# A graph network layer on one core: 21 dense blocks instead of 18, and all five extra groups built in the second layer

## The reference, cut to what matters

```python
xn = _layernorm(x)
deg_out = segment_sum(edge_weight, src); deg_in = segment_sum(edge_weight, dst)
norm = edge_weight * rsqrt(deg_out[src] * deg_in[dst] + EPS)
h6 = relu(segment_sum((xn @ W6)[src] * norm[:, None], dst) + b6)
h7 = relu(segment_sum((h6 @ W7)[src] * norm[:, None], dst) + b7)
gnn = h7 @ Wp + bp
q, k, v = xn @ wq.T, xn @ wk.T, xn @ wv.T      # 4 heads of 64; k and v are layer-normed
mix = (q @ (k.T @ v / S)) @ wo.T + bo
x = x + gnn + mix
x = x + ffn(_layernorm(x))                      # 2 of 8 experts, picked once for all nodes
```

## Time and profile before

| | |
|---|---|
| time, median of 3 runs | 3923.15 us (3919.55 to 3930.97) |
| span of the profiled execution | 3561.3 us |
| own time of the profiled execution | not listed apart from the three runs |
| PE busy | 2813.0 us (79%) |
| DVE busy | 1936.5 us (54%) |
| ACT busy | 950.0 us (27%) |
| POOL busy | 2357.1 us (66%) |
| moved by DMA | 511.33 MB, mean 144 GB/s |

### The profile page before, as it was taken

How to read it: one execution, slowest core, us unless ns; L and a number is a source line. 1 busy time by engine, 2 the same in 40 slices (tenths; PEclk the granted TensorE clock), 3 DMA queues, 4 the chain that set the end, 5 groups by cost and what they waited for, 6 DMA issues and landing times.

```text
span 3561.3 us, 51404 instructions
## 1 busy us (share of the span) xinstructions
PE 2813.0 (79%) x15774; PEld 1830.9 (51%) x15774; DVE 1936.5 (54%) x5283; ACT 950.0 (27%) x3210; POOL 2357.1 (66%) x2283
## 2 busy tenths in 40 slices
PE   4565558998989889998953577888778868869998
PEld 4454425555556555655521345555546535545666
DVE  9999846787778777877752142222243242232334
ACT  6787642332333323332220020000020010012111
POOL 5776577777777777777765777777777777730000
PEclk8788979999999999999975799999989999989999
DMA  4110035555555555555555546566646646642221
GB/s 132 59 44 1 2 104 151 167 159 151 162 164 158 150 157 170 155 156 160 166 177 156 170 149 195 197 201 200 195 147 196 197 153 193 198 156 95 79 71 49
DMA packets 260757, 511.33 MB, mean 144 GB/s; under 512 B 64843, under 2 KB 138459, under 8 KB 260141
## 3 DMA queue, kind: packets, MB, share of 16 engines
q0 software_dynamic: 97920, 268.62, 26.0%
q1 hardware_dynamic: 156057, 232.90, 19.7%
q10 hardware_dynamic: 6500, 6.40, 0.5%
HBM read 398.63 MB, written 109.15 MB: 143 GB/s over the span
## 4 chain that ended last, share of the span: by engine, by line
POOL 32%; PE 25%; DVE 15%; issue 12%; DMA 10%; SPq 4%; DVEq 1%; ACT 1%; ACTq 0%; POOLq 0%
POOL ringb L1908 31%; PE ps L676 7%; DVE ab L1058 6%; PE ps L845 5%; PE ps L858 5%; DMA ringb<-t,src 4%; PE ps L653 3%; DVE ab L1056 3%; DMA ab<-in_x 2%; SPq L1969 2%; PE ps L637 2%; SPq L1964 1%; DMA ab<-ad 1%; DMA rsd_in<-rdi 1%; POOL ab L1881 1%
## 5 line engine op out<-in xcount | busy, mean ns | idle before, releaser
L1908 POOL DMA_INDIRECT ringb<-t,src x2040 | 2044.2, 1002 | 684.0 <-issue 604.2
L676 PE MATMUL ps<-xb,ab 125*128 125x256 f32 (+1 forms) x4100 | 1062.0, 399 | 23.0 <-DMA ab<-ad 20.9
L676 PEld LDWEIGHTS ps<-xb,ab 125*128 125x128 f32 x4100 | 796.6, 199 | 287.1 <-issue 103.1
L653 PE MATMUL ps<-mlb 128*125 128x350 f32 x1176 | 495.6, 512 | 127.8 <-DVE mlb L1250 82.5
L637 PE MATMUL ps<-ringb,Sb 128*32 128x257 f32 (+1 forms) x4080 | 348.8, 416 | 280.6 <-DMA ringb<-t,src 178.2
L1697 ACT ACTIVATE ab<-ps 125x300 f32 x637 | 284.3, 446 | 671.0 <-PE ps L653 617.1
L559 PE MATMUL ps<-ab 128*50 128x125 f32 x3240 | 245.9, 306 | 183.3 <-ACT ab L1624 127.6
L1881 POOL TENSOR_TENSOR ab<-ab,wn 128x100 f32<-128x100 f32 x202 | 276.4, 1374 | 126.4 <-DVE ab L1056 126.4
L653 PEld LDWEIGHTS ps<-mlb 128*125 128x125 f32 x1176 | 208.6, 201 | 281.7 <-DVE mlb L1250 163.7
L637 PEld LDWEIGHTS ps<-ringb,Sb 128*32 128x32 f32 x4080 | 83.3, 111 | 496.7 <-DMA ringb<-t,src 273.7
L559 PEld LDWEIGHTS ps<-ab 128*50 128x50 f32 x3240 | 207.8, 143 | 221.2 <-DVE ab L1058 189.2
(11 more groups left out here) (231 smaller groups left out, 2520.8 us busy)
## 6 DMA issues: line engine op xcount, KB each, us to landing
ad<-ab SPq DMA_DIRECT2D x200, 312.5 KB
ab<-ad SPq DMA_DIRECT2D x200, 312.5 KB
ringb<-t,src POOLq DMA_INDIRECT x2040
x2t<-mlb SPq DMA_DIRECT2D x13, 500.0 KB, 18.5
xb<-x2t SPq DMA_DIRECT2D x13, 500.0 KB, 8.2
xb<-in_x SPq DMA_DIRECT2D x10, 625.0 KB
t<-xb SPq DMA_DIRECT2D x10, 625.0 KB
kvb<-t SPq DMA_DIRECT2D x50, 125.0 KB
```

The source lines that it names most:

```text
L653: e.matmul(PS[(2, 7, 4, 5)[bank_of(t)]][0:R, 0:HR], low[:, slot_of(t), :], high[:, slot_of(t), :], start=True, stop=True).then_inc(s_bld, 1)
L676: ins = e.matmul(PS[3][:, 0:wd], lhs, X[0:R, k, 0:wd], start=k == 0, stop=k == NT - 1)
L1908: e.indirect_dma_start(msg[:, slot * QT + k, 0:width], None, table, bass.IndirectOffsetOnAxis(src[:, t:t + 1], 0)).then_inc(s_g[slot], 16)
```

## The change

`ND`, the dense chunks of 30 tiles, goes from 18 to 21, and a block is begun every 11 steps instead of 13. The gathered groups fall from 45 to 41, so that the first layer has 246 steps with a gather instead of 270 and the second 216 instead of 240; the tiles fall from 1620 to 1614. The five extra groups are other ones, and all of them are built in the second layer, four tiles a step over six steps, instead of three of the five at three tiles a step over eight. The first layer builds 630 tiles instead of 588 (two or three a step both times) and runs 1050 dense products instead of 900; the second builds 120 instead of 72 and runs 1300 instead of 1150. 21 blocks are stored and loaded instead of 20. A chunk of the second layer has 176/26 = 6.8 steps instead of 206/23 = 9.0. Keys and values: of every fourth node tile phases 2 and 3 share a step, which takes them 237 steps instead of 250. `X_AT` comes to the steps 234, 236 and 240 (before 237, 240, 244), the last clearing of a place to step 219 (before 246), the late weights to step 245 (before 262). The loop of the first layer has 251 steps instead of 274, the second 237 instead of 257. ACT's scaling of `X` takes five rows a step instead of four.

```diff
-ND = 18
+ND = 21
-NY = 3
-YB = 8
-GX = [17, 44, 7, 26, 35]
+NY = 5
+YB = 6
+GX = [4, 11, 18, 30, 35]
-PD = 13
+PD = 11
+KV_JOIN = 4
-KV_STEPS = NT * 5
+KV_AT, _s = {}, FIRST
+for _i in range(NT):
+    for _ph in range(5):
+        if _ph and not (_ph == 3 and _i % KV_JOIN == 0):
+            _s += 1
+        KV_AT.setdefault(_s, []).append((_i, _ph))
+    _s += 1
+KV_AT.setdefault(_s, []).append((NT, 0))
+KV_STEPS = _s - FIRST
+KV_I = {s: i for s, v in KV_AT.items() for i, ph in v if ph == 0}
...
             def kv(s):
-                n = s - FIRST
-                i, ph = divmod(n, 5)
+                for i, ph in KV_AT.get(s, ()):
+                    kv_phase(i, ph, s)
...
             def scale_rows(s):
-                for t in range(4 * s, min(4 * s + 4, NT)):
+                for t in range(5 * s, min(5 * s + 5, NT)):
```

More of the change, by code:

```diff
@@ L469, in kv_copied @@
         def kv_copied(s):
-            return min(max((s - FIRST) // 5 + 1, 0), NT)
+            return sum(1 for at, i in KV_I.items() if at <= s and i < NT)
         def hidden_issued(s):
@@ L570, in kv, with kv_phase @@
             def kv(s):
-                n = s - FIRST
-                i, ph = divmod(n, 5)
+                for i, ph in KV_AT.get(s, ()):
+                    kv_phase(i, ph, s)
+            def kv_phase(i, ph, s):
                 k = i % 2
@@ L581, in kv @@
                     ins.then_inc(s_kk, 1)
-                if n < 0 or i >= NT:
+                if i >= NT:
                     return
@@ L1099, in kv, with kv_phase @@
             def kv(s):
-                i, ph = divmod(s - FIRST, 5)
-                if s < FIRST or i >= NT:
-                    return
+                for i, ph in KV_AT.get(s, ()):
+                    if i < NT:
+                        kv_phase(i, ph)
+            def kv_phase(i, ph):
                 ps3 = PS[5][0:R, :].rearrange("p (a d) -> p a d", d=64)
@@ L1992, in sp_program @@
                     store_A(s // PD - 1, s % PD)
[L1993 to L1999, removed]
+                for i, ph in KV_AT.get(s, ()):
+                    if ph == 1 and i < NT - 2:
+                        kv_load(i + 2)
+                    if ph == 1:
+                        e.wait_ge(s_kxc, i + 1)
+                        e.dma_start(xtd[i // 4].rearrange("p (h n) -> p h n", h=2)[:, :, i % 4 * R:(i % 4 + 1) * R],
+                                    xT[:, i % 2, :, :]).then_inc(l_xs[i % 2], 16)
                 if s in X_AT:
```

## The result

The kernel after takes 3740.28 us (median of 4 runs, 3733.75 to 3752.44). The kernel before, measured with it, takes 3924.47 us (4 runs). The medians lie 184 us apart. The ratio is 0.9544, with a 95% interval of 0.9525 to 0.9564; the quotient of the two medians, 0.9531, lies inside it. I had forecast 3824 us, 99 us less, within 3725 to 3911; the likeliest case's own range, 3775 to 3865, did not hold it.

The account below looks back on a forecast made before the run. It took POOL's back-to-back gathers to bound both layers, with PE and the transfers close behind. Terms of -1, -76, -33 and +11 us gave -99: 3923 - 99 = 3824 us, range 3725 to 3911.

Parts of the forecast that it names:

- prologue -1: Degree pass ahead of the layers: one batch less of DVE work, 1.2 us, taken as -1.
- first layer -76: First layer: PE sets the pace, body 1274 us, layer 1408 instead of 1484; ends -128 and +81.
- second layer -33: Second layer: POOL's time falls to 1109 us, builds add 20 and loads 60, giving 1189 us.
- tail +11: Behind the second layer's last gather: the stream's last chunks end 20 steps later instead of 16, +11 us.
- rival B: Both layers: the gathers stay the bound, 3692 us and up to 3775 with one term; chance 0.17.
- 362 us lie around the span, and I leave them alone: Whole kernel: span 3561.3 us against a median of 3923.15; the difference was taken as outside it and unchanged.
- rival C: Second layer: the stream's load of x queues behind loads of A, PE no longer catches up; slower, 4011 us; chance 0.08.
- 24 steps at 5.02 us: Each layer: 96 gathers less at 1.255 us, 120 us off POOL.
- POOL's bound: First layer: what POOL's gathers alone would allow, -128 us, a body of 1222 us.
- 20 for builds: Second layer: 30 build steps of four tiles at 5.7 us instead of 5.02, +20 us; ends 0 and +36.
- 60 for loads: Second layer: loads of A stretch 160 steps by 0.43 us, of which the ring hides some; +60, ends 0 and 125.
- D's idle time of PE: First layer: PE's idle time stays so large that 1484 us remain; 3900 us, 3865 to 3911; chance 0.20.

Follow-up runs that it names:

- e3: Kernel after, but each load of a stored block in the second layer brings only the first half of its columns; 3718.6 us, ratio 0.9515.
- e8: Kernel after, but first-layer blocks are multiplied with 26 of the 50 node tiles only, 504 products fewer; 3716.59 us, ratio 0.9484.
- e10: Kernel after, but POOL issues two of the four gathers of a first-layer step from the seventh step on; 3621.87 us, ratio 0.9165.
- e4: Kernel before with only the joined phases 2 and 3 of every fourth key/value tile; 3913.02 us, ratio 0.9995.
- e5: Kernel before with only all five extra groups built in the second layer, four tiles a step over six steps; 3926.54 us, ratio 1.0025.
- e7: Kernel after, but POOL issues only two of the four gathers of each second-layer step; 3571.65 us, ratio 0.9103.
- e6: Kernel after, but each second-layer gather brings rows of 512 B instead of 1 KB; 3711.19 us, ratio 0.9458.
- e9: Kernel after, but each second-layer gather brings 64 rows instead of 128; 3760.64 us on a slower chip, ratio 0.9511.
- e11: Kernel after, but the second layer has half the gathers and 26 of 50 dense products of a block; 3547.73 us, ratio 0.8977.
- e2: Kernel after, but second-layer blocks are multiplied with 26 of the 50 node tiles only, 624 products fewer; 3724.8 us, ratio 0.9528.

## Why the prediction came out as it did

**The total was held by the range, the sum was not right.** Its four terms against the two profiles taken on one chip: prologue -1, measured -0.1; first layer -76, measured -95.3; second layer -33, measured -100.3; tail +11, measured +12.6. That the range held 3740 was luck in the main: this stretch of it, 3725 to 3775, was there for rival B alone, and B's full queue of POOL did not come.

**The step that failed first: "362 us lie around the span, and I leave them alone".** They did not lie around it. The span of the same program run again was 387 us longer, and that lies within the layers: 196 us in the first and 181 in the second, 11 behind them. The page came from an execution unlike the timed ones, and a span that is 9% under the median of the runs should have raised the question. All absolute numbers that I gave for a check (1408 and 1189 us, 5.4 us a step) were therefore wrong: 1576, 1297 and 6.0 were measured. By my own line ("wrong if steps of the second layer average over 6 us") steps of 6.00 and 6.03 us would speak for rival C. DVE's wait for x seems to fall, from the 249.9 us of the earlier trace rows to 107.3; against the kernel before run again it rose, from 41.2. But it did not reach the time: e3 brings it to 9.1 and gains 11 us, uncertain by 16.

**Removed work was priced too low.** I took 24 steps at 5.02 us, 120 us a layer. At the 6.22 and 5.84 us that a step takes in the kernel before run again it is 149 and 140 us. That is 49 of the 84 us that the forecast lacked; 47 more come from the added work of the second layer, charged too high, the first layer takes 10 back, and prologue and tail 2.

**First layer, added work.** I let PE pace it, with POOL's bound 52 us lower. (The terms that I put together there, 1193 + 81 + 78 - 76, give 1276 and not 1274.) The layer got 54 us dearer than its steps alone (246 x (6.44 - 6.22)), so about +54 against the +44 that lies between my -120 and my -76. The size was near; the reason was not. PE is busy 1279 of 1450 us, 88% and not over 90, at 0.95 and not near 1.0; 219 us of its products removed give 24 (e8), half the gathers 149 (e10). What the 54 us are made of stays open: keys, values, the rows of h6 and the turns are the same in number and fall on fewer steps, and builds and products are more.

**Second layer, added work.** I charged 20 for builds and 60 for loads, and 7 for longer gathers. The steps got dearer by 216 x (6.03 - 5.84), some 40 us in all. Builds: against e4, whose layers are those of the kernel before on a like chip, e5 has +24 us in the second layer and -10 in the first, near my +20 and the 7 that 48 builds were worth there. Loads: halving all of them gives 11 us, uncertain by 16, where I expected 30 to 60, and PE waited for loads by 14.4 us in all (0.4 in the second profile of the kernel after, before its weight loads). So +60 was too high, most likely by most of its size: the transfers do not set the step there. In the Trainium skill, "DMA: Bandwidth & Descriptors", section "Why a DMA increments its semaphore by 16 and not by 1", a transfer over 125 partitions would use five engines, by which I estimated 3815 to 3911 us. The time was 3740, so the estimate did not come true; how many engines a load used no run here shows. SP's queue was held for 45.84 us by 12 pieces, 3.8 each, against 34.64 for ten in the earlier trace rows, but the kernel before run again has this, 4.2 each:

```profile
2360.95 41.58 SPq L1969 DMA_DIRECT2D ab<-ad  x10
```

**What was right.** The size of the tail; its cause was not looked at. The joined phases at nothing (e4). The wait of DVE for the store of A, gone: before the clearing in the kernel after no wait for a store is named (15.6 us in four waits are "remote"), while the kernel before run again has one of 9.4 us (not 22.1). POOL's longer gathers where DVE builds one-hots, 1049 against 969 ns; in the first layer of the kernel after a gather that overlaps them by over 0.5 us takes 1236 ns on the mean, one beside an idle DVE 948. POOL's waits for PE, forecast as tens of us, are 254, but the kernel before has 264 when run again, so they are no sign of the change.

**The rivals.** B, the gathers stay the bound, had 0.17; its interval, 3692 to 3775, holds the result, and e7 and e10 show that the number of gathers limits both layers. But not in B's way: POOL's queue is not full, it waits 2 us at a time for PE. A, with 0.50, had PE as the pace of the first layer. D's idle time of PE did stay, 171 of 1450 us, and yet the layer got shorter. That PE could wait for nothing and still be slow was no rival at all, because nothing in the earlier trace rows shows it.

**What stays open.** What in a gather slows PE. Bytes and rows are excluded but for some 34 and 13 us (e6, e9), POOL's issue as a queue too. What is left comes with each gather whatever its length: POOL's issue of it, some 0.95 us each, and the 16 rises of its semaphore. The last column of the table and the counts behind it would fit the second: where the late events are, the trace holds a quarter to a third of the gathers' rises, and 24.9 of 32 in e7. That might also be the recording itself, for every run of this study for which a span is listed, the timed ones too, was recorded. Neither is shown. In the Trainium skill, "NOTIFIC — the notification-queue block", section "Overflow: three behaviours, one of which stalls the engine", the block that writes event records always holds its producers up rather than lose a record inside itself; the late semaphores and gaps without a wait would agree with that. That two thirds to three quarters of the gathers' rises are missing from the trace is not what the sentence tells, no run here shows the block's counter, and none was recorded otherwise. Why the execution behind the earlier trace rows escaped all this is not known either.

## What to carry to other kernels

Before a forecast, hold the span of the page against the median of the runs: where they were 9% apart here, the page was of another regime, and its idle times, chain and full queue were not those of the timed kernel; the durations of POOL's and DVE's single instructions carried over (a gather 963 and 967 ns). The chain names who ended last, not what the step would gain: here it gave PE 53%, while half of PE's dense products were worth 6 us and half of the gathers 173. In this kernel having fewer indirect transfers was the gain, and neither shorter rows nor shorter gathers did instead; before trying that elsewhere, leave out half of them once and look.

## What the runs showed of the hardware

- The number of gathers, not their bytes, holds the layers up (173 us for half the number, 34 and 13 for half the bytes in the second). At 0.63 to 0.68 gathers per us PE's semaphores rise 2.5 to 8.2 us late at the 90th percentile, and in the second layer PE has gaps within straight code; at 0.35 to 0.39 the gaps are gone and the lateness is 0.04 us (0.32 in e11). One execution with 0.74 and 0.78 gathers per us has neither.
- The granted clock (mean of a body) went with PE's own load: with half of the dense products it fell from 0.92 to 0.81 in the second layer (e2) and from 0.95 to 0.90 in the first (e8), with half the gathers it rose to 0.95 and 0.97.
- A gather of 64 rows costs POOL 927 ns and one of 128 rows 969: the issue is nearly a fixed price.
